# Low halves of the weights by an accumulating transfer and ScalarE instead of GpSimd's subtraction

## The reference

```python
xn = _layernorm(x)                       # x: 2 x 2048 x 512
# s: a state-space layer (16 states per channel): h = a_t * h + b_t over time, y = sum_n h * C + xn * D
s = _ssm_forward(xn, ...)
# g: a mixture of 8 experts, 2 per token, at most 1024 rows each, hidden size 2048
h  = gelu(einsum('ecd,edh->ech', disp, fc1_w) + fc1_b)
eo = einsum('ech,ehd->ecd', h, fc2_w) + fc2_b
g  = silu(gated sum of the two experts' rows)
out = x + s * g                          # all float32
```

## Time and profile before

| | |
|---|---|
| median of 3 runs | 2114.82 us (2114.29 to 2119.66) |
| the profiled execution's own time | 2111.89 us |
| its span, first to last instruction | 2110.1 us |
| busy: PE, DVE, POOL, ACT | 1883.4, 1823.3, 1314.4, 1230.0 us |
| main loop | from about 285 to 2010 us of the span |

### The profile page before, as it was taken

One profiled execution on the slowest core, in us unless ns is written; L12 is line 12 of the kernel. 1 busy time (PEld: TensorE's weight loads), 2 busy tenths in 40 slices (PEclk: granted clock), 3 DMA queues, 4 the chain that ended last, 5 costly groups with the idle time before them and its releaser, 6 DMA issues. The chain is left out here.

```text
span 2110.1 us, 30181 instructions
## 1 busy us (share of the span) xinstructions
PE 1883.4 (89%) x9032; PEld 1463.7 (69%) x9032; DVE 1823.3 (86%) x1959; ACT 1230.0 (58%) x1799; POOL 1314.4 (62%) x581
## 2 busy tenths in 40 slices
PE   6599839999999999999999999999999999999900
PEld 3233227888788788878788778887887788778800
DVE  6556549989998999888988998899889988998869
ACT  3268746566655665656566655665566656565433
POOL 1167758566856685668566856786578657766600
PEclk9799959999999999999999999999999999999955
DMA  8714364123522351135114421442144223522199
GB/s 286 257 41 122 82 222 94 65 70 130 120 65 70 131 121 63 65 137 116 66 61 144 100 81 60 145 96 85 60 142 99 78 67 125 116 68 73 34 303 380
DMA packets 88548, 244.78 MB, mean 116 GB/s; under 512 B 13169, under 2 KB 14193, under 8 KB 77169
## 3 DMA queue, kind: packets, MB, share of 16 engines
q1 hardware_dynamic: 70640, 207.30, 28.5%
q0 software_dynamic: 17536, 35.73, 9.3%
q10 hardware_dynamic: 256, 0.26, 0.1%
HBM read 171.56 MB, written 71.70 MB: 115 GB/s over the span
## 5 line engine op out<-in xcount | busy, mean ns | idle before, releaser
L1016 POOL TENSOR_TENSOR ub_sb<-u_sb,brow_sb 128x1024 f32<-128x1024 f32 x256 | 640.4, 2502 | 418.9 <-DVE a_sb L1106 416.1
L1106 DVE TENSOR_TENSOR_SCAN a_sb<-a_sb,state,ub_sb 128x512 f32<-128x512 f32 x512 | 885.4, 1768 | 10.5 <-issue 6.3
L772 PE MATMUL pm<-xTh,w1l 128*128 128x512 f32 x1024 | 423.7, 414 | 9.2 <-issue 5.0
L772 PE MATMUL pm<-w2h,hl 128*128 128x512 f32 x1024 | 423.9, 414 | 0.0
L774 PE MATMUL pm<-w2h,hh 128*128 128x512 f32 x1024 | 402.6, 393 | 0.0
L774 PE MATMUL pm<-xTh,w1h 128*128 128x512 f32 x1024 | 402.1, 393 | 0.0
L773 PE MATMUL pm<-w2l,hh 128*128 128x512 f32 x1024 | 399.4, 390 | 0.0
L773 PE MATMUL pm<-xTl,w1h 128*128 128x512 f32 x1024 | 398.6, 389 | 0.0
L1077 DVE SCALAR_TENSOR_TENSOR s_acc<-pt,ct_keep,s_acc 128x512 f32<-128x512 f32 x480 | 351.7, 734 | 23.4 <-PE pt L802 22.6
L920 ACT ACTIVATE a_sb<-delta_sb,neg_a_keep 128x512 f32<-128x512 f32 x512 | 330.1, 713 | 6.7
L802 PE MATMUL pt<-m_ident,a_sb 128*128 128x128 f32 x2048 | 307.8, 273 | 24.2 <-DVE a_sb L1106 16.7
(11 more groups left out here) (135 smaller groups left out, 1986.6 us busy)
## 6 DMA issues: line engine op xcount, KB each, us to landing
w_raw<-in_w SPq DMA_DIRECT2D x64, 1024.0 KB, 5.0
brow_sb<-b_chunks SPq DMA_DIRECT2D x128, 256.0 KB, 3.5
moe_rows<-zeros_sb SPq DMA_DIRECT2D x5, 2048.0 KB, 16.7
xin_sb<-in_x SPq DMA_DIRECT2D x8, 1024.0 KB, 6.3
xn_rows<-xn_sb SPq DMA_DIRECT2D x8, 1024.0 KB, 8.4
delta_chunks<-ln_sb SPq DMA_DIRECT2D x8, 1024.0 KB, 5.2
u_chunks<-u_now_sb SPq DMA_DIRECT2D x16, 512.0 KB, 4.9
delta_sb<-delta_chunks SPq DMA_DIRECT2D x8, 1024.0 KB, 8.2
```

Source lines behind the costliest of these rows:

```text
L772: pe.matmul(out, sl, mh, start=start, stop=False)
L1016: pool.tensor_tensor(ub[:, h], u[:, 2 * h:2 * h + 2, :], brow[:, m % 2:m % 2 + 1, :].to_broadcast([P, 2, CH]), ALU.mult).then_inc(s_["bmul ...
L1106: op = dve.tensor_tensor_scan(abuf[:, m, 2 * h + k, :], abuf[:, m, 2 * h + k, :], ub[:, h, k, :], state[:, ds(col, 1)], ALU.mult, ALU.add)
```

## The change

ScalarE now writes minus the rounded value into the low half's own buffer (`lo`), then the high half as before. GpSimd issues a transfer of 1 MB from `lo` onto `raw` that adds (SBUF to SBUF, 128 partitions x 8 KB); then `raw` holds what the rounding left. ScalarE rounds this into `lo` (`finish_w`) and signals `w_lo`. `finish_w(it, 0)` stands behind `exp(3)`, `finish_w(it, 1)` behind `exp(7)` and ahead of the gelus of group 1. In the tail the last 12 stores share one semaphore, which only makes room for the two new ones.

```diff
@@ scalar
             act.sem_inc(s_["w_hi"], 1)
+            act.sem_inc(s_["w_lo"], 1)
...
             def split_w(it, which):
-                hi = w1h if which == 0 else w2h
+                hi, lo = ((w1h, w1l), (w2h, w2l))[which]
                 act.wait_ge(s_["raw_in"], 16 * (2 * it + which) + 16)
                 act.wait_ge(s_["l1" if which == 0 else "l2"], 8 * it + 1)
+                act.activation(lo[:].rearrange("p k f -> p (k f)"), raw[:], ACT.Copy, scale=-1.0).then_inc(s_["w_neg"], 1)
                 act.activation(hi[:].rearrange("p k f -> p (k f)"), raw[:], ACT.Copy).then_inc(s_["w_hi"], 1)
+
+            def finish_w(it, which):
+                lo = (w1l, w2l)[which]
+                act.wait_ge(s_["w_rest"], 16 * (2 * it + which) + 16)
+                apart(act, s_["act_at"])
+                act.activation(lo[:].rearrange("p k f -> p (k f)"), raw[:], ACT.Copy).then_inc(s_["w_lo"], 1)
...
                         if i >= lag:
                             exp(i - lag)
+                        if i == lag + 3:
+                            finish_w(it, 0)
...
                             for i in range(LATE, 8):
                                 exp(i)
+                            finish_w(it, 1)
@@ gpsimd
                     def low(which):
-                        hi, lo = ((w1h, w1l), (w2h, w2l))[which]
+                        lo = (w1l, w2l)[which]
+                        pool.wait_ge(s_["w_neg"], 2 * it + which + 1)
                         pool.wait_ge(s_["w_hi"], 2 * it + which + 2)
-                        pool.tensor_tensor(lo[:].rearrange("p k f -> p (k f)"), raw[:], hi[:].rearrange("p k f -> p (k f)").bitcast(F32), ALU.subtract).then_inc(s_["w_lo"], 1)
+                        apart(pool, s_["pool_at"])
+                        pool.dma_start(raw[:], lo[:].rearrange("p k f -> p (k f)").bitcast(F32), accum_op=ALU.add).then_inc(s_["w_rest"], 16)
@@ tail
-        parts = " ".join(f"xs{p} y{p} out{p}" for p in range(NP))
+        parts = " ".join(f"xs{p} y{p}" for p in range(NP)) + " out0 out1 out2 out3 outs"
```

More of the change, by code:

```diff
@@ L663, in main_loop @@
         pt = psum("pt", [P, 4, 512])
-        s_ = sems("m_", """ident raw_in w_hi w_lo x_got0 x_got1 x_got2 x_got3 x_turned x_hi x_lo l1 gelu h_free l2
+        s_ = sems("m_", """ident raw_in w_hi w_neg w_rest w_lo x_got0 x_got1 x_got2 x_got3 x_turned x_hi x_lo l1 gelu h_free l2
             acc_free exp h_turned summed bmul scan b_in0 b_in1 d_in u_in0 u_in1 s_out0 s_out1 s_out2 s_out3
@@ L964, in _ @@
         def _(pool):
-            pool.sem_inc(s_["w_lo"], 1)
             pool.sem_inc(s_["bmul"], 4)
@@ L1155, in store @@
                 sp.wait_ge(s_["sum"], p + 1)
-                sp.dma_start(out[p].rearrange("(j p) d -> p j d", p=P), o[:, p % RING]).then_inc(s_[f"out{p}"], 16)
+                sp.dma_start(out[p].rearrange("(j p) d -> p j d", p=P), o[:, p % RING]).then_inc(s_[f"out{p}" if p < NP - RING else "outs"], 16)
             for p in range(RING):
@@ L1163, in _ @@
                     load(p + RING)
-            for p in range(NP):
+            for p in range(NP - RING):
                 sp.wait_ge(s_[f"out{p}"], 16)
+            sp.wait_ge(s_["outs"], 16 * RING)
         @block.scalar
```

## The result

The changed kernel takes 2149.9 us (median of 4 executions, 2147.96 to 2153.07) where the kernel before took 2114.6 (4 executions on the same chip, 2111.15 to 2119.66): 1.0168 times as long, 95% interval 1.015 to 1.0186. The profiled execution took 2147.96 us, its span is 2146.1, 36.0 us longer than that of before.

What follows compares the result with a forecast made beforehand. The prediction took TensorE as the bound, busy 1656.9 of 1690.0 us in the main loop. Terms of +36, -24, +8, +31 and +8 made +59 on 2111.9, giving 2171, stated as 2170 us; range 2105 to 2255.

Steps and rivals of the forecast that it cites:

- likeliest case: The forecast's own case for the whole kernel: L from 8 to 10.5, 2137 to 2220 us, chance 0.50.
- The chain to step 8: w2 in middle quarters, step-1 transposes to scans' end: 14.4 + L us; TensorE stalls by L - 7.9 per quarter.
- L: Time from issue to landing of the 1 MB adding transfer, in us; forecast 9.0, between the adds' rate and a plain load's.
- a landing under 7 or over 11 us: Sign in the changed profile, at the weight transfer, that the forecast landing of about 9 us was wrong.
- The estimate from the Trainium skill: Transfer's landing by two skill pages: 2.0 + 2 x 2.4 = 6.8 us, no step 8 stall, sum near 2116.
- Step 8, +36: TensorE's stall at step 8 in 32 quarters, waiting for scans behind w2's chain: 1.1 us each, +36 us.
- the +8 for contention: First quarters of chunks: two adds ahead and four stores beside the w2 transfer, 1 us each, +8 us.
- Release of GpSimd, -24: Main loop: without GpSimd's 64 subtractions, all 24.2 us of TensorE's waits for scans and sums go, -24 us.
- Cover of w1 in middle quarters: w1's low half in middle quarters: needed only behind step 15, so its transfer is hidden up to L of about 11.
- Start, +8: First w1 of all: one more copy, the transfer and one copy replace the subtraction before TensorE starts, +8 us.
- Second quarters, +31: Second quarter of each of 8 chunks: TensorE waits 3.9 us for w1, split behind `bias_part`, +31 us.
- the rival with L from 6 to 8: Whole kernel: gain and loss cancel, 2122 us at 7, 2098 to 2137 over the case; chance 0.18.

Runs made afterwards that it cites:

- e5: Changed kernel with w2's last copy (raw into the low half) made twice, one behind the other; 1.0353 of the time of the kernel before.
- e6: Changed kernel with w2's last copy moved behind the second pair of gelus of group 1; 1.0173 of the time of the kernel before.
- e10: Changed kernel without subtraction, transfer or last copy; the negative high halves stand in for the low halves; 0.9823 of the time of the kernel before.
- e9: Changed kernel with SyncE's load of the next bias row ahead of the w2 weight load instead of behind it; 1.0191 of the time before.
- e1: Changed kernel with ScalarE's split of the next w1 ahead of the last four bias rows instead of behind them; 1.0014 of the time before.
- e2: Changed kernel with only w2's low half by copy, transfer, copy, and w1's by GpSimd's subtraction as before; 0.9979 of the time before.
- e3: Changed kernel with only w1's low half by copy, transfer, copy, and w2's by GpSimd's subtraction as before; 1.0175 of the time before.
- e4: Kernel before plus ScalarE's negative copies and the stores' shared semaphore, with GpSimd still subtracting and no transfer; 0.9997 of the time before.

## Why the prediction was right in direction, and what of its sum was wrong

The time, 2149.9, lies in the likeliest case's range and 20 us under its number; the largest term was nevertheless wrong, and others made up for it.

- **The chain to step 8** had the right structure: 14.4 + L from the step-1 transposes to the scans' end gives 21.8 at the measured L of 7.4, and 22.1 were measured (1076.86 to 1098.98). One link was mispriced: the hand-over from ScalarE to GpSimd's issue takes 0.6 us (the copy ends at 1082.10, the issue starts at 1082.68), not 0.07. So the limit is at L of about 7.7, not 7.9. Last quarters bear it out: there w2's transfer takes 8.1 us in seven chunks, and TensorE waits 0.35 to 0.56 us at step 8; e5, with 2 us more in the chain, shows that little slack is left elsewhere.
- **L** is the mis-sized term: 9.0 forecast, 7.4 measured for w2 and 6.9 for w1. The prediction named a landing under 7 or over 11 us as a sign of being wrong; both came, the second in first quarters. And it took one L for all places. The step was the choice "between the adds' rate and a plain one's", 786 KB at 230 GB/s on top of the adds' 5.6 us. The trace shows how it lands: busy share of the DMA engines in 40 slices of 0.15 us, 1034 to 1040, while a transfer for w2 (issued at 1031.67) is under way, and from 1038.3 on a load of 256 KB (GB/s below):

```profile
DMA  0099009900990099009900999700017999600000
GB/s 0 0 601 273 0 0 437 437 0 0 382 492 0 0 382 492 0 0 382 492 0 0 164 437 164 109 0 0 0 41 232 423 410 382 246 14 0 0 0 0
```

  Bursts of 0.3 us every 0.6, full rate within, nothing between: 0.15 us x 874 GB/s is 131 KB per 0.6 us, 218 GB/s. The rate of this add was thus within about 5% of the 230 that I took; it was the fixed part that I had too large, since 1049 KB at 218 GB/s is 4.8 us and leaves 2.6 for issue and landing. Adding to a whole small add's 5.6 us counted its data, and whatever slows it, as overhead. The estimate from the Trainium skill in the prediction, from "DMA: Bandwidth & Descriptors" (Anatomy of one DMA) and "Collectives: The Full Stack" (The bandwidth ceiling), was 6.8 us: it agrees with the 6.9 and 7.4 here to within a tenth, and its rule that an add runs at half a copy's rate fits the 218 GB/s, half of the 437 inside a burst. What follows for step 8 of middle quarters (no stall) it had right as well. The total near 2116 that the prediction put beside it doesn't follow even from its own terms: -24 + 6 + 22 + 8 at L of 6.8 makes 2124.
- **Step 8, +36:** measured 12.7 us, and hardly any in middle quarters. 8.8 are in first quarters. In the one near 987 us the pair of scans takes 3.9 us instead of 2.45, beside a product of GpSimd which itself had waited 3.1 us for its row. That is what the +8 for contention stood for, found in another form. The 3.7 in last quarters are the forecast stall, at a landing of 8.1 us; in e6, where w2's last copy stands later, they are gone.
- **Release of GpSimd, -24:** at 23 of the 25 places where TensorE waited in the earlier trace rows it no longer waits for scans or sums (at six of the 23 it waits for w1 instead), and e10 shows 38 us of release, not 24, and more than the 33 that the prediction called the most there is. "The other 9 idle us have other causes and stay" was false.
- **Chunk starts, nothing forecast:** in the changed kernel the 7.8 of these idle us that lie there turned into 10.2 us of waits for w1, which I had called hidden up to L of 11 by looking at middle quarters alone. The landing there is 9.5 to 11.7 us, beside three other transfers.
- **Cover of w1 in middle quarters:** it ends near L of 8.5, not 11. The transfer is issued 10.6 us ahead of TensorE's product (1060.26 and 1070.84), where the subtraction started 13.1 ahead of it (1040.90 and 1053.97): it stands behind the products of GpSimd, which wait for scans that w2's chain has made later. By that, these quarters would have stalled too with the forecast 9.0. In e6 the issue is 13.1 us ahead again; in e9, at 8.6, TensorE's product follows the last copy by 0.13 us in third and last quarters, so that no cover is left.
- **Start, +8:** 7.3 measured. **Second quarters, +31:** 24.3 us of waits. With the measured landing there, 6.9, the forecast's chain gives 8 x 2.9 = 23 (991.08 + 3.84 + 0.07 + 6.9 + 0.07 + 1.92 = 1003.88, against 1000.99), so the term was right but for L. e1 took it away.
- **Not foreseen:** half clock behind stalls, +7.8; and the tail, +4.6. I had written that the tail does not change. It starts when the last adds have landed, and those stand on GpSimd behind the last product:

```profile
2025.29 2.40 POOL L1028 TENSOR_TENSOR ub_sb<-u_sb,brow_sb 128x1024 f32<-128x1024 f32 x1 [2.51 <-DVE a_sb L1118]
...
2042.85 1.56 POOL L999 DMA_INDIRECT moe_rows<-part,add_now  x1 [0.30 <-issue]
```

  The last add is issued 4.9 us after TensorE's last transposes (2037.99); before, the two were 1.8 apart (2008.41 and 2006.57). The product waits for scans, which are late in the last quarter as at step 8.
- **SyncE's queue:** the weight load and the row behind it did not have the cover I claimed for them: GpSimd's 137 us of waits for rows are new (2.3 before). They cost TensorE little, and to remove them (e9) gained nothing.

With L at 7.4, the prediction's own sum would have been -24 + 0 + 6.6 + 27 + 8 = +18, some 2130 (27 from eight times 991.08 + 3.84 + 0.07 + 7.4 + 0.07 + 1.92 less 1000.99). The 23 us of the +36 for step 8 that never came stood in for the clock, the tail and the chunk starts. It ended near by luck as far as that goes, and the rival with L from 6 to 8, whose landing is the one measured, was given 2098 to 2137, too low by those same terms.

## What to carry to other kernels

Look for the place where an operation has least cover, not at its typical one: w2's transfer, 7.4 us in 32 quarters, cost less than its release of GpSimd gave (e2 is 0.2% faster than before), w1's cost all of the loss, most of it at eight places where its input stands behind another wait, and splitting the change in two (e2, e3) shows that in two runs. An engine taken off the critical path releases more than the waits that name it; a run without the work at all (e10) tells what there is to be had before one chooses how to do it. A median over all transfers of a kind hides the few that land beside others, and those can be the ones that are waited for. Gains at two places in a chain don't add: moving w2's copy was worth nothing before w1's wait was dealt with, and 0.7% after.

## What the runs showed of the hardware

- A transfer of 1 MB that adds from SBUF to SBUF goes in bursts, 131 KB every 0.6 us (218 GB/s), and lands 6.9 us after its issue with nothing beside it, 7.4 with a 256 KB load on another queue issued 3.5 us behind it, 8.4 to 8.8 with the same load 0.1 to 0.3 us behind it (e9), and 9.5 to 11.7 beside three others at chunk starts; a plain load of 1 MB takes 4.8. Its issue holds GpSimd 0.9 us.
- Behind four of the eight stalls at second quarters (3.29 to 3.50 us of waiting for w1) the granted clock fell to 0.50 for 3 to 7 us, which made layer 1 1.5 to 2.9 us longer; behind the other four (1.42 to 3.28 us) it took 25.5 us as always. The length of the stall alone doesn't decide it: of two waits of 2.42 us at chunk starts one was followed by half clock (1397) and one not (746), in e4 a wait of 1.81 us was (1167). The average clock of the loop, 0.99, hardly shows it; the durations of single matmuls (0.63 against 0.39) do.
- GpSimd's tensor operations make VectorE's scans longer: 885.4 us for 512 before, 694.4 after, where of these only the products are left, 662.2 in e10, where the transfers are gone too. That the last 32 us are the transfers' doing is not shown.
